# Gated cross-attention and quantised MLP block: variance before the last maximum, split steps alternated, and one of four tiles summed on TensorE

## The reference

```python
x = x + tanh(g_xattn) * (ctx @ Wv @ Wout + bout)
h = layernorm(layernorm(x)) * ln1_g + ln1_b         # the second norm rescales only
h = quant(h) @ ternary(w1).T + b1                   # quant: scale by 127 / max|row|, round
h = gelu(h)
h = layernorm(h) * ln2_g + ln2_b
h = quant(h) @ ternary(w2).T + b2
x = x + tanh(g_ffn) * h
```

## Time and profile before

| | |
|---|---|
| median of 3 runs | 412.6 us (412.28 to 414.04) |
| the profiled execution | 411.33 us, of it 409.5 us from the first to the last instruction |
| busy: PE, DVE, ACT, POOL | 309.5, 327.3, 277.6, 221.4 us |
| mean granted TensorE clock | 0.946 of full speed |

### The profile page before, as it was taken

How to read it: one execution, slowest core, us unless ns; L and a number is a source line. 1 busy time by engine, 2 the same in 40 slices (tenths; PEclk the granted TensorE clock), 3 DMA queues, 4 the chain that set the end, 5 groups by cost and what they waited for, 6 DMA issues and landing times.

```text
span 409.5 us, 5758 instructions
## 1 busy us (share of the span) xinstructions
PE 309.5 (76%) x1658; PEld 186.5 (46%) x1658; DVE 327.3 (80%) x794; ACT 277.6 (68%) x446; POOL 221.4 (54%) x117
## 2 busy tenths in 40 slices
PE   2846777687969697979797969797979684938365
PEld 2744643343636363636363636363636341515043
DVE  0345461998999999999999999999999996968681
ACT  1202237598887878787888888787878776969421
POOL 4000416577566666666666666666666666664600
PEclk9988889998999999999999999999999996969688
DMA  7941223316365555556555555555552526353625
GB/s 225 378 149 47 81 91 108 89 51 115 117 116 169 113 170 112 171 104 182 108 175 107 178 105 179 103 179 104 128 101 81 101 79 88 93 96 86 153 53 154
DMA packets 98557, 51.59 MB, mean 126 GB/s; under 512 B 87407, under 2 KB 89640, under 8 KB 98526
## 3 DMA queue, kind: packets, MB, share of 16 engines
q1 hardware_dynamic: 96608, 51.00, 49.1%
q10 hardware_dynamic: 1918, 0.23, 0.4%
HBM read 21.78 MB, written 8.46 MB: 74 GB/s over the span
## 4 chain that ended last, share of the span: by engine, by line
DVE 41%; PE 30%; issue 12%; POOL 7%; DMA 5%; ACT 3%; DVEq 0%; POOLq 0%; ACTq 0%
DVE y L657 10%; PE bank_f L904 8%; POOL rstd L295 6%; PE slot_c L864 5%; DVE h L616 5%; DVE amax L624 5%; DVE res L707 5%; PE slot_a L890 4%; DVE amax L661 3%; DMA split_vectors<-vec_parts 3%; PE slot_b L890 3%; DVE x L573 2%; DVE parts L559 2%; PE slot_a L887 2%; PE bank_q L794 2%
## 5 line engine op out<-in xcount | busy, mean ns | idle before, releaser
L311 POOL TENSOR_TENSOR y<-u,g_bc 128x1024 f32<-128x1024 f32 x64 | 150.2, 2369 | 28.7 <-DVE parts L559 25.4
L295 POOL TENSOR_TENSOR rstd<-var,half_neg 128x8 f32<-128x8 f32 x18 | 30.3, 1683 | 129.5 <-DVE var L698 86.1
L657 DVE TENSOR_TENSOR y<-y,slot_c 128x1024 f32<-128x1024 f32 x64 | 77.6, 1212 | 5.0 <-PE slot_c L864 5.0
L661 DVE TENSOR_REDUCE amax<-y 128x1 f32<-128x1024 f32 x64 | 78.1, 1220 | 2.2
L441 ACT ACTIVATE junk<-u,usum 128x1024 bf16<-128x1024 f32 x64 | 73.7, 1151 | 1.2
L414 ACT ACTIVATE q<-y,s 128x1024 f16<-128x1024 f32 x64 | 69.8, 1139 | 5.2 <-DVE s L688 5.0
L843 PE MATMUL bank_q<-wvo,ctxT 128*128 128x256 f32 x256 | 69.1, 402 | 0.0
L904 PE MATMUL bank_f<-w2T,q2T 128*128 128x256 f16 x512 | 64.1, 281 | 0.0
L904 PEld LDWEIGHTS bank_f<-w2T,q2T 128*128 128x128 f16 x512 | 51.5, 101 | 14.3 <-issue 0.8
L405 ACT ACTIVATE q<-h,s 128x256 f16<-128x256 f32 x64 | 27.3, 496 | 41.2 <-DVE s L648 41.1
L864 PE MATMUL slot_c<-ln_rows,rows 128*128 128x512 bf16 x128 | 40.9, 402 | 16.9 <-DVE y L657 8.5
(11 more groups left out here) (104 smaller groups left out, 393.1 us busy)
## 6 DMA issues: line engine op xcount, KB each, us to landing
c_in<-in_ctx SPq DMA_DIRECT2D x16, 512.0 KB, 3.3
x_in<-in_x SPq DMA_DIRECT2D x16, 512.0 KB, 4.6
out<-res SPq DMA_DIRECT2D x32, 256.0 KB, 2.4
y<-in_L_ffn_w SPq DMA_DIRECT2D x2, 1024.0 KB, 12.1
u<-in_L_xattn_Wkv SPq DMA_DIRECT2D x1, 1024.0 KB, 7.0
u<-in_L_xattn_Wout SPq DMA_DIRECT2D x1, 1024.0 KB, 10.6
q2T<-q SPq DMA_TRANSPOSE x64, 3.3
g_bc<-in_L_ffn_ln_g SPq DMA_DIRECT2D x1, 512.0 KB, 12.4
```

The lines of the kernel that those rows point to most:

```text
L295: nc.gpsimd.tensor_tensor(rstd[:, :, :], var[:, :, :], half_neg[:, :, :], ALU.pow) \
L311: nc.gpsimd.tensor_tensor(y[:, k % 2, t, :], u[:, t, :], g2_bc[:, :], ALU.mult).then_inc(gain2_done, 1)
L657: nc.vector.tensor_tensor(line, line, slot_c[:, :], ALU.add).then_inc(y_done, 1)
L661: nc.vector.tensor_reduce(amax2[:, t:t + 1], y[:, k % 2, t, :], AX.X, ALU.max, apply_absolute_value=True).then_inc(amax2_done, 1)
```

## The change

`variance` of set i moves from the start of the next body into body i, behind `join`, and both come before the maximum of the first norm (L624). POOL's `root` therefore moves from the start of a body to the end of the one before, and `rstd` gets two buffers. The split steps stand one by one between residual, statistics and final steps. `correction`, `row` and their semaphore counts lose tile 0: TensorE's new `head` sums that tile in `slot_a`, by its terms (bf16, as before) and a product of the unit matrix with y in fp32, both halves of 512 columns, behind shift_first and before the second half of turn_context; DVE's `row_max(0)` and ACT's `quantise(k, 0)` read `slot_a`, and hidden 0 of the next body waits for that. `take_context` moves on ACT: the first in front of gelu 1, the second behind square 3. In places where `rstd[:, 0, :]` or `rstd[:, 1, ...]` was read, `rstd[:, i % 2, ...]` is read; most of these lines are left out of the diff below.

```diff
@@ -286,13 +287,14 @@
-                def root():
-
-                    wait(pool, var1_done, min(i + 2, S))
-                    wait(pool, var2_done, i)
-                    wait(pool, first_ready, min(i + 1, S))
-                    wait(pool, second_ready, i - 1)
-                    nc.gpsimd.tensor_tensor(rstd[:, :, :], var[:, :, :], half_neg[:, :, :], ALU.pow) \
+                def root(j):
+
+                    wait(pool, var1_done, min(j + 2, S))
+                    wait(pool, var2_done, j)
+                    wait(pool, first_ready, min(j, S))
+                    wait(pool, second_ready, j - 2)
+                    nc.gpsimd.tensor_tensor(rstd[:, j % 2, :, :], var[:, :, :], half_neg[:, :, :],
+                                            ALU.pow) \
...
@@ -306,13 +308,15 @@
 
-                    wait(pool, q2_done, T * (k - 2) + t + 1)
+                    if t == 0:
+                        wait(pool, head_done, k - 1)
+                    else:
+                        wait(pool, q2_done, T * (k - 2) + t + 1)
                     wait(pool, gelu_done, T * k + t + 1)
                     nc.gpsimd.tensor_tensor(y[:, k % 2, t, :], u[:, t, :], g2_bc[:, :],
                                             ALU.mult).then_inc(gain2_done, 1)
 
                 if -1 <= i <= S:
-                    root()
                     wait(pool, split_steps, split_count(i))
                 if i == -1:
                     pool.wait_ge(g1_in, 16)
@@ -326,6 +330,8 @@
                 if live(i):
                     gain(i, 0)
                     gain(i, 1)
+                if -1 <= i + 1 <= S:
+                    root(i + 1)
 
             for i in bodies:
                 body(i)
@@ -411,14 +417,15 @@
-                    nc.scalar.activation(q2[:, t, :], y[:, k % 2, t, :], ACT.Copy,
-                                         scale=s2[:, t:t + 1]).then_inc(q2_done, 1)
+                    nc.scalar.activation(q2[:, t, :], y[:, k % 2, t, :] if t else slot_a[:, :],
+                                         ACT.Copy, scale=s2[:, t:t + 1]).then_inc(q2_done, 1)
 
                 def take_rows():
 
                     wait(act, rows_done, i + 2)
                     wait(act, shift1_done, min(i + 1, S))
-                    wait(act, corr_done, T * (i - 1))
+                    wait(act, corr_done, 3 * (i - 1))
+                    wait(act, head_done, i - 1)
                     wait(act, hid_done, T * min(i, S))
                     wait(act, ffn_done, T * (i - 2))
                     nc.scalar.copy(rows[:, :, :].rearrange("p a n -> p (a n)"),
@@ -462,18 +469,17 @@
                 if live(i):
                     gelu(0)
                     square(0)
-                    gelu(1)
                 if live(i + 3) and i > -3:
                     take_context(i + 3, 0)
                 if live(i):
+                    gelu(1)
                     square(1)
                     gelu(2)
-                if live(i + 3) and i > -3:
-                    take_context(i + 3, 1)
-                if live(i):
                     square(2)
                     gelu(3)
                     square(3)
+                if live(i + 3) and i > -3:
+                    take_context(i + 3, 1)
 
             for i in bodies:
                 body(i)
...
@@ -576,19 +583,21 @@
 
-                def statistics(k, h):
-
-                    wait(dve, x1_done, 2 * k + h + 1)
-                    wait(dve, join_steps, 3 * k)
-                    nc.vector.bn_stats(bn[:, 2 * h, :], x1[:, k % SETS, 2 * h, :])
-                    nc.vector.bn_stats(bn[:, 2 * h + 1, :], x1[:, k % SETS, 2 * h + 1, :]) \
-                        .then_inc(bn_done, 1)
+                def statistics(k, t):
+
+                    if t % 2 == 0:
+                        wait(dve, x1_done, 2 * k + t // 2 + 1)
+                        wait(dve, join_steps, 3 * k)
+                    op = nc.vector.bn_stats(bn[:, t, :], x1[:, k % SETS, t, :])
+                    if t == T - 1:
+                        op.then_inc(bn_done, 1)
 
                 def join(k, n):
 
                     if n == 0:
-                        wait(dve, bn_done, 2 * k + 2)
-                        wait(dve, split_steps, split_count(k - 2))
+                        wait(dve, bn_done, k + 1)
+                        wait(dve, std_done, i + 2)
+                        wait(dve, split_steps, split_count(i))
                         nc.vector.tensor_tensor(mean1[:, :], bn[:, :, 1], bn[:, :, 4], ALU.add)
                         nc.vector.tensor_tensor(gap1[:, :], bn[:, :, 1], bn[:, :, 4], ALU.subtract)
                         nc.vector.tensor_tensor(var[:, 0, :], bn[:, :, 2], bn[:, :, 5], ALU.add) \
...
@@ -646,19 +655,23 @@
+                            out=s1[:, :], in0=amax1_inv[:, :], scalar=QMAX * TINY,
+                            in1=rstd[:, i % 2, 0, :], op0=ALU.mult, op1=ALU.mult).then_inc(first_ready, 1)
 
                 def row(k, t):
 
                     line = y[:, k % 2, t, :]
-                    wait(dve, corr_done, T * k + t + 1)
+                    wait(dve, corr_done, 3 * k + t)
                     wait(dve, gain2_done, T * k + t + 1)
                     nc.vector.tensor_tensor(line, line, slot_c[:, :], ALU.add).then_inc(y_done, 1)
 
                 def row_max(k, t):
-                    wait(dve, y_done, T * k + t + 1)
-                    nc.vector.tensor_reduce(amax2[:, t:t + 1], y[:, k % 2, t, :], AX.X, ALU.max,
+                    if t == 0:
+                        wait(dve, head_done, k + 1)
+                    else:
+                        wait(dve, y_done, 3 * k + t)
+                    nc.vector.tensor_reduce(amax2[:, t:t + 1],
+                                            y[:, k % 2, t, :] if t else slot_a[:, :], AX.X, ALU.max,
                                             apply_absolute_value=True).then_inc(amax2_done, 1)
 
                 def second(k, n, those=slice(0, T)):
...
@@ -687,27 +700,28 @@
+                            in1=rstd[:, i % 2, 1, those], op0=ALU.mult, op1=ALU.mult) \
                             .then_inc(second_ready, 1)
 
                 def variance(k):
 
                     wait(dve, square_done, T * k + T)
-                    wait(dve, split_steps, split_count(k))
+                    wait(dve, std_done, i + 2)
...
@@ -716,41 +730,60 @@
                     dve.wait_ge(tanh_done, 1)
-                if live(i - 1):
-                    variance(i - 1)
+                splitting = -1 <= i <= S + 1
+                if -1 <= i <= S:
+                    deviations()
+                if splitting:
+                    split(0)
                 if live(i + 2):
                     residual(i + 2, 0)
+                if splitting:
+                    split(1)
+                if live(i + 2):
                     statistics(i + 2, 0)
                 if i == -2:
                     scale_weights(1)
                     round_weights(1, 0)
-                if -1 <= i <= S:
-                    deviations()
-                if -1 <= i <= S + 1:
-                    for n in range(5):
-                        split(n)
+                if splitting:
+                    split(2)
+                if live(i + 2):
+                    statistics(i + 2, 1)
+                if splitting:
+                    split(3)
                 if live(i - 3):
-                    final(i - 3, 1)
+                    final(i - 3, 2)
+                if splitting:
+                    split(4)
+                if live(i - 3):
+                    final(i - 3, 3)
                 if live(i + 2):
                     residual(i + 2, 1)
-                    statistics(i + 2, 1)
+                    statistics(i + 2, 2)
+                    statistics(i + 2, 3)
                 if live(i - 1):
-                    row(i - 1, 0)
-                    row_max(i - 1, 0)
                     row(i - 1, 1)
                     row_max(i - 1, 1)
                     if i == S:
+                        row_max(i - 1, 0)
                         for n in range(4):
                             second(i - 1, n, slice(0, 2))
                     row(i - 1, 2)
                     row_max(i - 1, 2)
+                    row(i - 1, 3)
+                    row_max(i - 1, 3)
                 if live(i - 2):
                     final(i - 2, 0)
-                if live(i - 1):
-                    row(i - 1, 3)
-                    row_max(i - 1, 3)
+                    final(i - 2, 1)
                 if live(i + 1):
                     shift_first(i + 1)
+                if live(i - 1) and i < S:
+                    row_max(i - 1, 0)
+                for n in range(4):
+                    if live(i + 2):
+                        join(i + 2, n)
+                if live(i):
+                    variance(i)
+                if live(i + 1):
                     first(i + 1, 0)
                 for n in range(4):
                     if i == S:
@@ -759,8 +792,6 @@
```

(60 more changed lines are left out.)

15 lines of the change are left out of this document (6 added, 9 removed).

## The result

The changed kernel takes 426.4 us (median of 4 runs, 425.19 to 428.15) against 412.4 us (median of 4 as well). The ratio is 1.0345 with a 95% interval of 1.0313 to 1.0377: slower, as forecast (423.8 us, range 411 to 431), by 13.9 us where 11.2 were forecast. The profiled execution took 428.15 us with a span of 426.4 us, 1.8 us above the median and the slowest of its four, where the profiled one before was the fastest; what follows in the trace adds up to 16.9 us between the two spans.

The account below looks back on a forecast made before the run. DVE was taken to set the pace (20.56 us per body), PE's line afterwards (21.0). Start +4.0, 13 bodies +5.7 and end +1.5 gave +11.2 on 411.33, 422.5; with 1.3 for the median 423.8 us, range 411 to 431.

Parts of the forecast that it names:

- The head's price: On PE, the head's two fp32 products of 512 columns take 0.86 us each, 1.72 together; bounds 0.43 and 2.2.
- Steps 1 to 6: Steady body followed from one L648 to the next, through corrections, PE's unbroken line and head; 21.0 us against 20.56.
- PE's 19.1 us of busy time: Sign to look for in a steady body: PE busy about 19.1 us.
- The hidden split steps were not on the path after all: Steady body: DVE is ready by about 4.9 us, row 1 starts at 4.97, so alternating the split steps shortens nothing.
- The read of `slot_a` costs like one of SBUF: DVE's maximum of tile 0 needs no longer from PSUM; the skill's figure would add 0.065 us, 1 us in all.
- Vector steps don't overlap: Rival on DVE: alternated split steps still cost about 0.25 us each, 6.5 us more, 430 in all; chance 0.02.
- The head is hidden or cheap: Rival: PE's line at least 1.0 us shorter, ACT's loop sets the body at 19.5, time 401 us; chance 0.14.
- Gain and loss cancel: Rival: PE's line 0.4 us shorter per body, start and end half as dear, 411 to 414.7 us; chance 0.10.
- the dear case at 430: The rival that vector steps don't overlap: row 1 some 0.5 us later per body, 430 us; chance 0.02.
- The start, the term that was mis-sized: Start up to body 1's first_ready: first product 1 us earlier, then +2.2 and +2.8; sum +4.0, bounds 0 and +6.
- The 1 us by which the first product was to come earlier: Start: shift_first now stands ahead of a context transpose that waited 2.84 us for ACT; first product 1 us earlier.
- The end, mis-sized too: Last bodies: root and a row leave the path, the head costs up to 4.3 us at 1.2 GHz; +1.5, bounds -3, +4.

Follow-up runs that it names:

- e8: Changed kernel with the fp32 product of the head done twice; 451.6 us (one run).
- e3: Changed kernel with the five split steps in one run behind residual(0) and its two statistics; 426.0 us, ratio 1.0342.
- e7: Changed kernel with variance, root and join back in their old places and the split steps in one run; 424.5 us, ratio 1.0292.
- e1: Changed kernel with the head's product in bf16, reading truncated upper halves of y; 412.4 us, ratio 0.998.
- e9: Changed kernel with fp16 head and join ahead of shift_first, and POOL waiting for join before its multiplication of tile 1; 404.4 us, ratio 0.9797.
- e11: e10 with body 0's second context copy ahead of gelu 3 and its transposes ahead of hidden 3; 400.9 us, ratio 0.9727.
- e5: Changed kernel without head, old order of second product 0, correction 3, finals and row 3 from i = 14; 411.5 us, ratio 0.9949.
- e10: e9 with the old order of second product 0, correction 3, finals and row 3 from i = 15; 402.4 us, ratio 0.9748.
- e12: e11 with tile 0 of y and the unit matrix in fp32 again; 416.3 us, ratio 1.0077.
- e4: Changed kernel with the four join steps moved ahead of shift_first; 415.1 us, ratio 1.0074.
- e6: Changed kernel with tile 0 of y in fp16, summed by an fp16 unit matrix, and join ahead of shift_first; 412.2 us, ratio 0.9986.
- e2: Changed kernel without the head: tile 0 has correction, row and maximum again, correction 3 stands before the second product; 414.1 us, ratio 1.0035.

## Why the prediction was right

The direction and the mechanism of the steady body were right, the size a little low: 13.9 us by the medians for 11.2, and 16.9 between the profiled executions. The steady bodies come out as forecast (0.36 us each for 0.44); what is missing lies at the start and at the end. That the forecast is only 2.6 us from the median, where the profiled execution is 5.7 us from the 422.5 of the sum, is in part luck: 1.3 us had been added for the median, and the traced execution was the slowest of its four.

- **The head's price** (1.72 us for the product, taken from the row of 256 columns): 0.86 per half in the trace, and e8 puts 1.73 on the body for a second one.
- **Steps 1 to 6**: correction 1 at 4.24 for 4.3, correction 3 at 8.63 for 8.70, head at 14.04 for 14.12, body 20.92 for 21.0. The waits of 1.0 and 1.0 were 0.92 and 0.86. PE's 19.1 us of busy time was 18.44; before it was 17.32, so it rose by 1.12 and not by 1.72. That records of overlapping matmuls count once is a likely reason, not a shown one.
- **"The hidden split steps were not on the path after all"**: e3, 0.03 us. With variance and root back in their old places (e7) DVE comes late to row 1 again, 0.92 us later than here.
- **The read of `slot_a` costs like one of SBUF**: the maximum takes 1.22 to 1.23 from PSUM and 1.22 from SBUF. By the table of the Trainium skill (VectorE: DVE Perf Modes, section on the TRN2 errata) the difference would be 0.065 us, an estimate from its 120 and 58 cycles; here it is at most 0.01.
- **Vector steps don't overlap** (rival): the residual starts 0.11 us behind a split step of 0.22 (183.91, 184.02). The Trainium skill (same page, The DRAIN you can't avoid) says that the next operation waits until the pipe is empty, but adds that one that is not held starts earlier, which I had left out; the trace shows the earlier start.
- **The head is hidden or cheap** (rival): e1 shows what it would have given. The body would be 20.0 and not 19.5: the wait for shift_first (0.92) and join behind it stayed. With the cheap head and join early and undisturbed ACT's loop takes over, at 19.26 (e9).
- **Gain and loss cancel** (rival): a slip in the sum. 412.6 + 0.5 + 2 is 415.1, above the 414.7 given for it; and the dear case at 430 lies inside the range that was to leave it out. Neither bears on the result.
- **The start, the term that was mis-sized**: +4.0 up to the third first_ready was +5.2 (98.21 for 93.04). The squares in front of variance cost the 2.2 forecast (77.05 for 74.55, less the 0.27 below), and the next body 2.7 for 2.8 (21.16 for 18.49). The 1 us by which the first product was to come earlier did not come: ACT's first gelu, which waits for it, starts 0.27 us later. ACT's timeline before, and after:

```profile
64.40 1.11 ACT L433 ACTIVATE u<-slot_a,d 128x1024 f32<-128x1024 f32 x1 [2.47 <-PE slot_a L890]
```

```profile
64.67 1.12 ACT L440 ACTIVATE u<-slot_a,d 128x1024 f32<-128x1024 f32 x1 [2.38 <-PE slot_a L935]
```

  So the first first_ready is 2.9 us earlier and the first product is not. This makes the +10.1 of the three bodies look larger than the loss: at the fourth first_ready the kernel is 7.2 us late (120.79 for 113.61). The third of these bodies lasted 22.58 instead of 21.0 because its attention ran at the lower clock in this execution; in e3, with the same order there, it ran at the full clock and the body took 20.93. PE's timeline after, and of e3:

```profile
99.59 1.88 PE L874 MATMUL bank_q<-wvo,ctxT 128*128 128x256 f32 x4
```

```profile
100.39 1.03 PE L865 MATMUL bank_q<-wvo,ctxT 128*128 128x256 f32 x4
```

  In e7, with variance back, the first body is 2.9 us shorter (22.20 to 19.33), but the next one loses 2.0 of it again (21.16 to 23.13). There DVE's residual waits for the attention, which stands behind the context copy after the squares:

```profile
78.40 0.75 DVE L579 SCALAR_TENSOR_TENSOR x<-bank_q,tg,x_in 128x512 f32<-128x512 f32 x1 [3.79 <-PE bank_q L862]
```

  In e11, with that copy early, it is the other way round: the attention waits 3.78 for the residual behind variance. By these waits the two chains are about equally long, which would be why taking back one alone shows little. A kernel with both taken back was not tried, and how the 7.2 us divide between them and the clock is open.
- **The end, mis-sized too**: +1.5 was +4.95 in the profiled execution. I costed the head at the lower clock there, 1.2 GHz (a row of its fp32 product took 1.91 for 1.02, at 397.54), but set the gains of root and row almost wholly against it. e1 differs in nothing but that product, and its end is 48.8 us, no longer than before (49.1): about 5 us of the end go with the fp32 product, give or take the 2 us by which this stretch varies. I also overlooked that correction 3 now stands ahead of the second product: in body 16 that product starts 32.9 us after the last first_ready (405.25 less 372.36), behind a correction that waited 3.16. e5 and e10 put the old order back, and their medians are 2.6 and 2.0 us lower; only for e5 is that clear of the noise. With the head in fp32 the old order (e12) has an end of 52.3 us, the new one (e4) of 54.0.

## What to carry to other kernels

Work taken from the busiest engine is worth nothing until the new chain is followed from one semaphore to the next: here 1.25 us of vector work per body went (DVE busy for 18.07 us of a body, 19.32 before), and an fp32 product at the end of another engine's line took it back with what stood behind it. Put steps that need nothing from the late result ahead of the wait for it. And when a tiny instruction moves, look what POOL does at that moment. Judge a new order at the start and at the end too, from more than one execution: with one order the same stretch differed by 1 to 2 us.

## What the runs showed that I had not expected

A vector step of 128x4 elements with both inputs in SBUF took 1.18 us (0.15 alone) and ended with POOL's running multiplication; one wait on POOL gave 0.70 us per body back and 8 us in all (e6 to e9). The runs also show that a kernel whose steady body is 0.57 us shorter need not be faster over its whole length: the start and the end of a deep pipeline weighed 10.8 us in the profiled executions of e2 and before, and about 6.4 by their medians.
